# Scatters of a mixture of experts: eight plain rows a token in place of four accumulated ones

## What is computed

```
xn = layernorm(x)
x  = x + attention1(xn) + moe(xn)
moe: 64 experts; each token takes 8 of them (4 of 8 groups, then the top 8 of their biased scores)
     out[token] = sum over its 8 experts e of  weight[token, e] * (silu(xn @ wg[e].T) * (xn @ wu[e].T)) @ wd[e].T
```

## Time and profile before

| what | value |
|---|---|
| median of the runs | 1225.39 us |
| the profiled execution, its time | 1228.2 us |
| its span, first to last instruction | 1226.4 us |
| PE busy in the span | 1092.7 us, 89% |
| DVE busy | 691.8 us, 56% |
| ACT busy | 645.8 us, 53% |
| POOL busy | 546.0 us, 45% |
[...]

### The profile page before, as it was taken

One profiled execution on the slowest core, in us unless ns is written; L12 is line 12 of the kernel. 1 busy time (PEld: TensorE's weight loads), 2 busy tenths in 40 slices (PEclk: granted clock), 3 DMA queues, 4 the chain that ended last, 5 costly groups with the idle time before them and its releaser, 6 DMA issues. The chain is left out here.

```text
span 1226.4 us, 25064 instructions
## 1 busy us (share of the span) xinstructions
PE 1092.7 (89%) x7538; PEld 655.3 (53%) x7538; DVE 691.8 (56%) x2408; ACT 645.8 (53%) x1336; POOL 546.0 (45%) x520
## 2 busy tenths in 40 slices
PE   6679999999999999998995999988988888988983
PEld 3346666666666565646663555444444444444552
DVE  6486565656566666624584656454445454454526
ACT  4215454555555545474464786665555755565640
POOL 3332222222221000003103687787877787777851
PEclk9899999999999999999897999999999998899996
DMA  7401141214121402021145659757686657875568
GB/s 237 86 27 47 30 84 31 64 31 83 31 65 32 76 25 70 19 71 40 36 130 159 168 112 226 148 99 189 110 232 131 119 111 168 187 165 105 94 121 287
DMA packets 104013, 130.16 MB, mean 106 GB/s; under 512 B 32583, under 2 KB 81991, under 8 KB 103880
## 3 DMA queue, kind: packets, MB, share of 16 engines
q1 hardware_dynamic: 68550, 77.46, 22.5%
q0 software_dynamic: 30720, 47.21, 21.6%
q10 hardware_dynamic: 4616, 3.91, 1.0%
HBM read 89.18 MB, written 38.97 MB: 104 GB/s over the span
## 5 line engine op out<-in xcount | busy, mean ns | idle before, releaser
L688 DVE CUSTOM_DVE_ANT_0 a_masked<-a_ps_s,a_mask 128x512 bf16<-128x512 f32 (+3 forms) x512 | 229.9, 487 | 158.7 <-PE a_ps_s L847 154.9
L1593 POOL DMA_INDIRECT y<-e_y,dst x160 | 256.5, 1603 | 76.9 <-issue 39.9
L604 ACT ACTIVATE a_probs<-a_ps_e 128x512 f32<-128x512 f32 (+1 forms) x384 | 188.3, 527 | 120.9 <-PE a_ps_e L867 119.9
L1816 PE MATMUL e_ps_gu<-e_w_gu,e_xT 128*64 x640 | 217.7, 485 | 1.1 <-DVE e_xT L1684 1.1
L1816 PE MATMUL e_ps_gu<-e_s_gu,e_xT 128*64 128x352 f32 x640 | 217.7, 485 | 0.0
L186 POOL DMA_INDIRECT yn<-rows,inv x160 | 158.6, 991 | 117.5 <-DVE inv L1405 58.9
L1841 PE MATMUL e_ps_y<-e_w_d,e_hT 88*64 x640 | 154.6, 385 | 19.7 <-issue 17.7
L1623 ACT ACTIVATE e_y<-e_ps_y,e_weight 128x256 f32<-128x256 f32 x160 | 75.0, 470 | 161.9 <-DMA y<-e_y,dst 144.0
L1841 PE MATMUL e_ps_y<-e_s_d,e_hT 88*64 88x256 f32 x640 | 154.8, 385 | 0.0
L864 PE MATMUL a_ps_e<-a_qT,a_kT 75*128 75x512 bf16 (+3 forms) x512 | 140.8, 303 | 2.1 <-ACT a_probs L604 1.8
L847 PE MATMUL a_ps_s<-a_kT,a_qT 72*128 72x512 bf16 (+3 forms) x512 | 131.2, 300 | 12.5 <-DVE a_headmax L688 11.3
(11 more groups left out here) (234 smaller groups left out, 1808.1 us busy)
## 6 DMA issues: line engine op xcount, KB each, us to landing
e_w_gu<-e_gu SPq DMA_DIRECT2D x64, 352.0 KB
e_w_d<-e_down SPq DMA_DIRECT2D x64, 176.0 KB
a_qT<-qk_parts SPq DMA_DIRECT2D x48, 192.0 KB
y<-a_mask SPq DMA_DIRECT2D x17, 512.0 KB, 5.5
e_w_gu<-y SPq DMA_DIRECT2D x5, 1024.0 KB
qk_parts<-a_stage SPq DMA_DIRECT2D x16, 256.0 KB, 2.6
e_w_d<-y SPq DMA_DIRECT2D x3, 1024.0 KB
yn<-rows,inv POOLq DMA_INDIRECT x160, 3.0
```

Source lines behind the costliest of these rows:

```text
L604: nc.scalar.activation(probs[:, i % HKV, UCOL[u]:UCOL[u + 1]], ps_e[:, (i * 3 + u) % 2, 0:w], ACT.Exp, scale=SCALE0).then_inc(exp_done, 1)
L688: ins = V.tensor_tensor_reduce(masked[:, n % 2, c:c + w], ps_s[:, n % 2, c:c + w], mask[:, T - w:T], 1.0, -3e38, ALU.add, ALU.max, headmax ...
L1593: pool.indirect_dma_start(t["y4"], bass.IndirectOffsetOnAxis(dst[:, j:j + 1], 0), y[:, j % NY, :], None, compute_op=ALU.add).then_inc(y_ou ...
L1816: ins = nc.tensor.matmul(ps_gu[r * SEG:(r + 1) * SEG, j % 2, 0:2 * INTER1], xT[:, j // 2 % 2, j % 2, k * P + r * SEG:k * P + (r + 1) * SEG ...
```

## The change

- `y4` becomes `y8` with a row for every (token, choice), 16384 rows, and one row for every padding slot behind them. A scatter is a plain one and waits for no other. The zeroing of `y4` in layer 0 goes.
- Routing needs the rank (0 to 7) of each slot beside the token. The products of rank k go to a PSUM region of their own, `inverse(k)`, two in each of four banks; PE zeroes the four banks first with four products. DVE adds the eight regions with weights 4 to the k (one copy and seven more steps on PSUM), and reads token and rank off the bits.
- The largest second-smallest slot of a token (`latest`) goes to HBM and back (SP, at experts 9 and 15), and at block 100 DVE works out from it how many scatters must have landed before ranks 6 and 7 of all tokens are there. With the given inputs that slot lies in block 106.
- After the weights, SP waits for the attention of three of the four position groups (block 116 or so) and for those scatters, and loads ranks 6 and 7 of the 12 token tiles of these groups (3.1 MB) over the keys and values of the attention, which are no longer needed.
- At the end SP reads tile by tile, 16 transfers: six rows a token for those 12 tiles (0.79 MB each) and eight for the other four (1.05 MB each), together 13.6 MB. There are 8 buffers; from tile 8 on, a read waits until the tile eight before is finished.
- Tiles 1, 4, 7, 10, 12 and 14 are added up on PE (8 products each), the other ten on DVE (three or four folds and the addition to x).

```diff
@@ -62,6 +61,8 @@
 
 
 
+EARLY_ROWS, EARLY_BATCHES = 2, 3
+EARLY_TILES = tuple(i for i in range(NT) if i % TPB < EARLY_BATCHES)
 SCATTERS = 8
 
 SCRATCH = {
@@ -69,9 +70,10 @@
     "qk_parts": ((B, NP_ * 2 + 2, P, T), BF16),
 
     "rows": ((TOK + P, ROW), F32),
-    "y4": ((PARTS * (TOK + P), D), F32),
+    "y8": ((TOK * TOPK + NLOAD * P, D), F32),
     "segments": ((4 * P,), I32),
     "segments_f": ((4 * P,), F32),
+    "latest": ((P,), F32),
 }
 
...
@@ -388,15 +390,8 @@
                     load_k(sp, m // TPB)
                 if NQ <= m < STEPS:
                     load_q(m)
-                if n == 0:
-                    sp.wait_ge(mask_in, 16)
-                if n <= NT:
-                    sp.dma_start(t["y4"].rearrange("(n p k) d -> n p k d", p=P, k=PARTS)[n],
-                                 mask[:, 0:D].rearrange("p (k d) -> p k d", k=1).to_broadcast([P, PARTS, D]))\
-                      .then_inc(y4_clear, 16)
             late.load(sp, t, late_in)
             sp.wait_ge(late_in, late.COUNT * 16)
-            sp.wait_ge(y4_clear, (NT + 1) * 16)
 
         ON_DVE = (0, 2, 3)
...
@@ -1209,7 +1207,9 @@
         block = ctx.enter_context(nc.Block())
 
         SELECTED, SPREAD = 8, 12
-        inverse = ps_inv[:, 3, 0:NLOAD]
...
@@ -1375,6 +1376,7 @@
             ch.step(V.tensor_scalar(pos_i[:, 1, :], slot_i[:, :], 7, None, ALU.logical_shift_right))
             V.tensor_copy(pos2[:, :, :, :], pos_i[:, :, :].rearrange("p a (j r) -> p a j r", r=1)
                           .to_broadcast([P, 2, NT * 8, 2])).then_inc(pos_ready, 1)
+            ch.did(V.tensor_reduce(latest[:, :], v8[:, :, TOPK - EARLY_ROWS], AX.X, ALU.max))
...
@@ -1395,22 +1397,24 @@
 
                     dve.wait_ge(oh_used, (i - NOH + 1) * EIGHT)
                 equal(oh_b[i % NOH], 1, i, NLOAD, oh_ready)
+            ch.did(V.tensor_scalar(pad_row[:, :], iota[:, :], float(P), pad_id[:, 1:2], ALU.mult, ALU.add))
             dve.wait_ge(oh_used, NT * 8)
 
-            ch.step(V.tensor_copy(code[:, :], inverse))
+            ch.step(V.tensor_copy(code[:, :], inverse(0)))
+            for k in range(1, EIGHT):
+                ch.step(V.scalar_tensor_tensor(code[:, :], inverse(k), 4.0 ** k, code[:, :], ALU.mult, ALU.add))
             ch.did(V.tensor_scalar(is_pad[:, :], code[:, :], 0.0, None, ALU.is_equal))
             bits = code[:, :].bitcast(I32)
             ch.step(V.tensor_scalar(token[:, :], bits, 13, 2 * 1024 - 1,
                                     ALU.logical_shift_right, ALU.bitwise_and))
             V.scalar_tensor_tensor(inv[:, :], is_pad[:, :], pad_id[:, 0:1], token[:, :],
                                    ALU.mult, ALU.add).then_inc(inv_ready, 1)
-            ch.step(V.scalar_tensor_tensor(row[:, :], is_pad[:, :], pad_id[:, 0:1], token[:, :], ALU.mult, ALU.add))
-            by_parity = (x.rearrange("p (j a) -> p j a", a=2) for x in (dst[:, :], row[:, :]))
-            place, source = by_parity
-            for a in range(2):
-                ch.did(V.tensor_scalar(place[:, :, a], source[:, :, a], float(PARTS), pad_id[:, 1 + a:2 + a],
-                                       ALU.mult, ALU.add))
-            ch.last()
+            ch.did(V.tensor_scalar(rank[:, :], bits, 24, None, ALU.logical_shift_right))
+            ch.step(V.tensor_tensor(pad_row[:, :], pad_row[:, :], is_pad[:, :], ALU.mult))
+            ch.step(V.scalar_tensor_tensor(row[:, :], token[:, :], float(TOPK), rank[:, :],
+                                           ALU.mult, ALU.add))
+            ch.step(V.scalar_tensor_tensor(dst[:, :], row[:, :], -60.0, pad_row[:, :],
+                                           ALU.add, ALU.add))
 
         @block.tensor
...
-                nc.tensor.matmul(inverse, oh_p[:, i % 2, k, :], oh_b[i % NOH][:, k, :],
-                                 start=(j == 0), stop=(j == NT * 8 - 1), skip_group_check=True).then_inc(oh_used, 1)
+                nc.tensor.matmul(inverse(k), oh_p[:, i % 2, k, :], oh_b[i % NOH][:, k, :],
+                                 start=False, stop=(i == NT - 1), skip_group_check=True).then_inc(oh_used, 1)
                 if k == EIGHT - 1:
                     qkv_part(SPREAD + i // 4, i % 4 // KD, i % KD)
 
 
-def layer1_experts(nc, t, ident, late, ring, x_sb, qkv1, seg_expert, expert_f, inv, dst, last):
+def layer1_experts(nc, t, ident, late, ring, x_sb, qkv1, seg_expert, expert_f, inv, dst, last, latest):
 
 
     ctx = ExitStack()
     with ctx:
         NS, NW, NY, NQ = ring.NS, ring.NW, SCATTERS, 8
         PAIRED = NBLK // 2
-        LEAD, BEHIND = 2, 4
...
@@ -1514,23 +1525,46 @@
 
         spare_gu = w_gu[:, 0:NW - 1].rearrange("p s k i -> p (s k i)")
         spare_d = w_d[:, 0:NW - 1].rearrange("p s k d -> p (s k d)")
-        TWO = 2 * PARTS * D
-        y4 = [spare[:, f * TWO:(f + 1) * TWO].rearrange("p (i k d) -> p i k d", i=2, k=PARTS)
-              for spare, n in ((spare_gu, 5), (spare_d, 3)) for f in range(n)]
-        rows4 = t["y4"][0:TOK * PARTS].rearrange("(i p k) d -> p i k d", p=P, k=PARTS)
+        y8 = [spare[:, f * TOPK * D:(f + 1) * TOPK * D] for spare, n in ((spare_gu, 5), (spare_d, 3)) for f in range(n)]
+        LATER = TOPK - EARLY_ROWS
+        rows8 = t["y8"][0:TOK * TOPK].rearrange("(i p k) d -> i p k d", p=P, k=TOPK)
+        early8 = qkv1[:, :, 3 * D - EARLY_ROWS * D:3 * D]
+        spare = seg_expert[0:1, 3 * P:4 * P].bitcast(F32)
+        scattered = seg_expert[0:1, 3 * P - 1:3 * P]
         filled = seg_expert[0:1, 3 * P - 1 - NY:3 * P - 1]
         ps_turned, ps_out = (ps_yT, ps_hT), (ps_o, ps_xT)
         (summed, o_added, x_done_a, x_done_b, stored) = sems(
             ctx, nc, "e_summed", "e_o_added", "e_x_done_a", "e_x_done_b", "e_stored")
-        ON_PE = (NT - 2, NT - 1)
-        ON_DVE = range(NT - 2)
-
-        def landed(eng, f):
-            eng.wait_ge(w_in[f], NE // ring.FIRST * 32 + 16)
+        early_in, = sems(ctx, nc, "e_early_in")
+        EARLY_COUNT = 32 + len(EARLY_TILES) * 16
+
+        def landed_y8(i):
+
+            return w_in[i % NF], NE // ring.FIRST * 32 + (i // NF + 1) * 16
+
+        ON_PE = (1, 4, 7, 10, 12, 14)
+        ON_DVE = [i for i in range(NT) if i not in ON_PE]
 
         def done_of(i):
 
-            return (x_done_b, ON_PE.index(i) + 1) if i in ON_PE else (x_done_a, i // 2 + 1)
+            return (x_done_b, ON_PE.index(i) + 1) if i in ON_PE else (x_done_a, ON_DVE.index(i) + 1)
+
+        def add_up(eng, E, i, ch, done):
+
+            f = i % NF
+            eng.wait_ge(*landed_y8(i))
+            def fold(n, other):
+                ch.step(E.tensor_tensor(y8[f][:, 0:n * D], y8[f][:, 0:n * D], other, ALU.add))
+
+            if i in EARLY_TILES:
+                fold(EARLY_ROWS, early8[:, i, :])
+                fold(LATER - 4, y8[f][:, 4 * D:LATER * D])
+            else:
+                fold(4, y8[f][:, 4 * D:8 * D])
+            fold(2, y8[f][:, 2 * D:4 * D])
+            fold(1, y8[f][:, D:2 * D])
+            eng.wait_ge(o_added, ON_DVE.index(i) + 1)
+            E.tensor_tensor(x_sb[:, i, :], x_sb[:, i, :], y8[f][:, 0:D], ALU.add).then_inc(done, 1)
 
         def gate_up_copied(j):
...
@@ -1553,25 +1587,44 @@
 
         @block.sync
         def _(sp):
-            def weights_in(e):
+            def landed(e):
                 sp.wait_ge(w_in[e % ring.FIRST], (e // ring.FIRST + 1) * 32)
                 sp.sem_inc(w_ready, 1)
 
             for e in range(ring.FIRST - 1):
-                weights_in(e)
+                landed(e)
             for e in range(ring.FIRST, NE):
                 if e >= NW:
                     blocks = sp.value_load(last[0:1, e - NW:e - NW + 1], min_val=1, max_val=NBLK)
                     sp.wait_ge(y_ready, blocks)
                 ring.load(sp, t, e)
-                weights_in(e - 1)
-            weights_in(NE - 1)
+                landed(e - 1)
+                if e == ring.FIRST + 1:
+                    sp.dma_start(t["latest"].rearrange("(p a) -> p a", a=1), latest[:, :],
+                                 allow_slow_non_contiguous=True).then_inc(early_in, 16)
+                if e == NW - 1:
+                    sp.wait_ge(early_in, 16)
+                    sp.dma_start(spare, t["latest"].rearrange("(a p) -> a p", a=1)).then_inc(early_in, 16)
+            landed(NE - 1)
+
+            sp.wait_ge(y1_ready, EARLY_BATCHES * B)
+            first_rows = sp.value_load(scattered, min_val=16, max_val=NBLK // NY * 16)
+            for b in range(NY):
+                sp.wait_ge(y_out[b], first_rows)
+            for i in EARLY_TILES:
+                sp.dma_start(early8[:, i, :].rearrange("p (k d) -> p k d", d=D), rows8[i, :, LATER:TOPK, :])\
+                  .then_inc(early_in, 16)
 
             counts = [sp.value_load(filled[0:1, b:b + 1], min_val=16, max_val=NBLK // NY * 16) for b in range(NY)]
             for b in range(NY):
                 sp.wait_ge(y_out[b], counts[b])
-            for f in range(ring.FIRST):
```

(56 more changed lines are left out.)

38 lines of the change are left out of this document (27 added, 11 removed).

## The result

The kernel before took 1226.47 us (median of 4 runs, 1225.15 to 1231.42), the changed one 1150.19 us (4 runs, 1147.43 to 1151.07): ratio 0.9367, 95% interval 0.9336 to 0.9399. The prediction was 1159.5. The profiled execution of the changed kernel took 1147.43 us, with a span of 1145.6 us against 1226.4.

The account below looks back on a forecast made before the run. POOL's accumulating scatters were taken to bound the experts' stage (3.17 us a block against PE's 2.635). Terms -82.9 + 14 + 2 + 1 = -66 us gave 1159.5 us; own range 1145 to 1172, up to 1200 for 8 in 10.

Parts of the forecast that it names:

- The scatter's price: Experts' stage, POOL: a plain scatter takes 0.99 us like the gather, so a block costs POOL 2.58 us, under PE's 2.635.
- Rivals 1 and 2: POOL: plain scatter as costly as the accumulating one, median 1234 (chance 0.12); or in between, 1.3 us, median 1181 (0.12).
- The stage at PE's pace: Experts' stage: 79 pairs at 5.27 us, 416.3 against 499.2 measured, -82.9 us; with stalls added, net -68.9.
- (a): Stall in the experts' stage: four exponentials make ACT load its tables, 4 x 1.25 = +5 us.
- (b): Stall in the experts' stage: DVE's attention pieces 7 and 8 overrun the pair by 0.7 us; +4 us (0 to 8).
- (c): Experts' stage: POOL's 2% margin, early loads sharing DMA with gathers near block 117, DVE's block-100 instructions; +5 us (0 to 12).
- The wait that goes: Experts' stage, POOL: scatter j no longer waits for j-2; with 3.6 us to landing it hardly ever held, worth 0.
- Routing: Before the experts' stage: extra PE and DVE steps make `inv` later by 3.4 us, the barrier by +2 us (1 to 4).
- Zeroing: Layer 0: 17 pieces of 512 KB no longer written; 0, at best -3 us.
- The end: After PE's last down product: DVE's folds set the end, reads hidden; 48 us against 47.2 before, +1 us.
- Rival 4: Early rows come late: at worst 3.1 MB more at the end, 8 us, half under DVE, 1164; no separate chance given.
- Rival 3: Experts' stage: another wait (late gathers, DVE or ACT) replaces POOL's; pairs of 5.7 us, +34 us, median 1194; chance 0.08.

Follow-up runs that it names:

- the third measurement: The changed kernel unaltered, run once more on chip 11: 1152.9 us (6 runs), ratio 0.939 to the kernel before.
- the good run: The first profiled execution of the changed kernel, unaltered, against the kernel before: 1147.43 us, span 1145.6 us against 1226.4.

## Why the prediction held, step by step

*The scatter's price.* Forecast 0.99 us on POOL, measured 1006 ns in the mean. The row chosen, the gather, was the right one, and the kernel before with plain scatters shows that this term alone gives the whole gain (-82 us of 1226.75). Rivals 1 and 2 are out. POOL's row ends before the data land: 0.99 us, and 3.2 to the landing (median, 2.4 to 6.6). The plain scatter's median, 988 ns, is 0.63 of the accumulating one's 1577 and within 2 ns of the gather's 990. What POOL does in that time no run shows, only that it is busy. In the sum of DMA time holds nine scatters and not ten, 1.1 us each; a plain one takes a third of that, and the conclusion, that DMA doesn't bound the stage, stands.

*The stage at PE's pace.* Forecast 416.3 + 14 = 430.3 us, measured 420.2. This is where the forecast was 10 us too slow. Of its three allowances (a) was right, 4 x 1.23 (ACT loads a table before each exponential and one behind it, 1.28 us each); (b) and (c), +4 and +5, cost nothing (the last two, shorter pairs give 0.9 back). For (b) the timeline of DVE in such a pair in the changed kernel:

```profile
862.35 0.69 DVE L1734 COPY e_xT<-e_ps_xT 128x512 f32<-128x512 f32 x1 [0.97 <-PE e_ps_xT L1856]
...
868.05 0.69 DVE L1734 COPY e_xT<-e_ps_xT 128x512 f32<-128x512 f32 x1
```

The pair does take DVE 5.70, 0.43 over PE's 5.27, but ahead of it DVE had idled 0.97, and what it is late with is needed a pair later. Here a single overrun of 0.43 us with 0.97 of idle time ahead of it cost nothing; it was counted as if it were lasting. (c) is the same mistake with the transfers: the gathers' lead took all of it, and the early loads only started at 1039, when the weights' loads were through, not at block 117.

*The wait that goes.* Forecast 0, because landings take 3.6 us; the waits of before have it once, for 1.6 us. This step was wrong. 3.6 us is the least that the trace shows of these landings (median 4.1, up to 8.7), and the gaps that the table puts down to ACT hold 13.6 us of this wait in the first 140 scatters; without it, and with scatters as slow as before, the stage is 10.7 us shorter. With plain scatters the one before the last was issued 5.1 us ago and not 6.3, and some land only after 6.6 us: kept, the wait goes with 9.0 + 2.8 us on chip 10, and 4.6 in the kernel before with plain scatters. The sum was not hurt, since it took PE's pace for granted. That was lucky: with the wait left in, the same sum would have come out, and PE's pace would not quite have held.

*Routing.* Forecast +2 at the first pair; measured -1.2 (675.20 for 676.41), and +4.2 in the third measurement (680.58). Most of the 5.4 us between the two goes with the clock. At nearly the same clock (0.81 and 0.83 from 575 to 600 us, before and in the third measurement of the changed kernel) POOL's first instruction of layer 1 and `inv` are 89.6 us apart before and 92.7 after: +3.1, against +3.4 forecast for `inv`, and the first pair is 3.2 us later by the same count. The 1 to 4 us of the range hold it.

*Zeroing.* Forecast 0, at best -3. Neither shown nor excluded.

*The end* (T is PE's last down product). Forecast T + 48, measured T + 47.1; folds 32.5 forecast, 32.4 measured; reads from T - 7 forecast, T - 9.4 measured. That the reads hide behind DVE's work is shown by two kernels: with more to read 0.2 us are lost, with DVE's folds begun earlier 2.0 are gained. The sign "DVE without gaps from the last down product on" did not come: it idles 0.66 us before each addition of attention but the first, and 1.1 before PE's first tile.

*Rival 4*, early rows that come late, did not happen: they were issued at 1039. It would have cost less than the 4 us that it was given, since without any early rows the end is 0.2 us longer.

*Rival 3* had 34 us in store for pairs of 5.7, and came on chip 8 with 124 us, though not for a reason it named: the gathers, the scatters and DVE's work are as long there as in the good run. As a forecast for that chip the prediction is wrong.

## What to carry to other kernels

Look at what the issuing engine itself spends on its transfers. In the kernel before POOL issued indirect transfers without a pause, and its own rows were the bound, 3.17 us a block against PE's 2.635; a row cost 1.58 us where the transfer accumulates and 0.99 where it doesn't, and eight plain rows a token came out cheaper than four accumulated ones (1150 against 1226 us). When a bound goes, reread each wait at the new pace, and don't read it off the table alone: where the engine named had long been done (22 us, in the case of block 45), another wait held, there a landing. Here such a wait held POOL for 13.6 us and was taken for nothing. And measure a kernel whose engines follow each other within a few per cent (2.57 and 2.635 us a block) on more than one chip before its gain is believed: the ratio was 0.939 on chip 11 and 1.040 on chip 8.
